# Keys with the four column positions innermost, ACT's norm in the second pair of a row, and a loop of two samples a turn (two turns) in place of one sample (five turns)

## What is computed

```
x = x + window_attention(group_norm(x))
x = x + lif(group_norm(x) @ W.T + b)          # over the 8 samples as time steps
# window_attention: windows of 8 x 8 positions, 16 heads of 16 channels
qkv  = part @ qkv_w.T + qkv_b ;  q = q * 16 ** -0.5
attn = softmax(q @ k.T + bias[rel_index] + mask)
out  = attn @ v
# group_norm: 32 groups of 8 channels, mean and variance over a sample's positions
# lif: v = v + (h - v) / 2 ; s = (v >= 1) ; v = v * (1 - s) ; output s
```

## Time and profile before

| | |
|---|---|
| median of 3 runs | 545.47 us (545.28 to 548.49) |
| the profiled execution | 546.64 us; its span 544.9 us |
| busy PE (matmul), PEld (weight load) | 434.2, 403.4 us |
| busy DVE, ACT, POOL | 398.2, 377.4, 280.3 us |
| queue of SP's DMAs | 154272 packets, 64.52 MB, 46.4% of 16 engines |
| packets under 512 bytes | 124978 of 155272 |
| granted TensorE clock | mean 0.962 of full speed |

### The profile page before, as it was taken

How to read it: one execution, slowest core, us unless ns; L and a number is a source line. 1 busy time by engine, 2 the same in 40 slices (tenths; PEclk the granted TensorE clock), 3 DMA queues, 4 the chain that set the end, 5 groups by cost and what they waited for, 6 DMA issues and landing times.

```text
span 544.9 us, 20474 instructions
## 1 busy us (share of the span) xinstructions
PE 434.2 (80%) x7912; PEld 403.4 (74%) x7912; DVE 398.2 (73%) x838; ACT 377.4 (69%) x863; POOL 280.3 (51%) x382
## 2 busy tenths in 40 slices
PE   0056658889878986988698879889988887889997
PEld 0056558878868886978698779778888776778886
DVE  5753757777776877677767767778877676588897
ACT  2353657878886887678778867788888786756551
POOL 6163456556654766475647654765685556640000
PEclk9996979999998999899989988999999998899999
DMA  7232534556554555455545654565555453023333
GB/s 204 67 81 65 140 75 107 142 142 155 138 139 109 141 138 137 109 128 142 138 114 133 139 131 112 129 140 134 123 118 119 111 125 80 2 78 136 135 137 135
DMA packets 155272, 65.78 MB, mean 121 GB/s; under 512 B 124978, under 2 KB 142644, under 8 KB 155188
## 3 DMA queue, kind: packets, MB, share of 16 engines
q1 hardware_dynamic: 154272, 64.52, 46.4%
q10 hardware_dynamic: 916, 0.01, 0.1%
HBM read 39.33 MB, written 25.17 MB: 118 GB/s over the span
## 4 chain that ended last, share of the span: by engine, by line
PE 38%; SPq 21%; ACT 11%; DMA 10%; issue 9%; DVE 8%; ACTq 1%; POOL 0%; DVEq 0%; POOLq 0%
SPq L317 12%; SPq L311 7%; DMA k_stack<-k_spill0lo 4%; PE pv_ps L1050 4%; PE proj_ps L939 3%; DMA k_stack<-k_spill1lo 3%; PE proj_ps L940 3%; PE proj_ps L941 3%; PE score_ps L1026 3%; PE score_ps L1016 3%; PE proj_ps L926 3%; PE pv_ps L926 3%; PE score_ps L926 3%; ACT xn L493 2%; ACT v_hi L529 2%
## 5 line engine op out<-in xcount | busy, mean ns | idle before, releaser
L454 POOL TENSOR_TENSOR p_lo<-probs,p_hi 128x512 f16<-128x512 f32 x128 | 146.4, 1165 | 147.3 <-ACT p_hi L608 122.9
L1016 PE MATMUL score_ps<-q_stack,k_stack 96*128 96x64 f16 x1024 | 88.1, 197 | 50.5 <-ACT max_rows L598 39.2
L1016 PEld LDWEIGHTS score_ps<-q_stack,k_stack 96*128 96x128 f16 x1024 | 74.2, 100 | 56.8 <-ACT max_rows L598 47.7
L785 DVE TENSOR_REDUCE neg_max<-max_ps 128x16 f16<-128x1024 f32 x64 | 78.4, 1225 | 42.9 <-PE max_ps L996 41.3
L607 ACT ACTIVATE probs<-score_ps 128x512 f32<-128x512 f32 x128 | 76.9, 601 | 38.4 <-PE score_ps L1026 37.6
L779 DVE TENSOR_TENSOR v_lo<-proj_ps,v_hi 64x256 f16<-64x256 f32 x128 | 54.2, 423 | 59.3 <-ACT v_hi L529 58.4
L939 PE MATMUL proj_ps<-xn_hi,w_hi 128*128 128x256 f32 x256 | 76.8, 300 | 10.7 <-DVE w_lo L738 7.2
L1012 PE MATMUL score_ps<-both_parts,bias_k 128*128 128x64 f16 x1024 | 80.8, 197 | 0.0
L608 ACT ACTIVATE p_hi<-score_ps 128x512 f16<-128x512 f32 x128 | 77.3, 604 | 0.0
L1012 PEld LDWEIGHTS score_ps<-both_parts,bias_k 128*128 128x128 f16 x1024 | 72.8, 100 | 2.8
L940 PE MATMUL proj_ps<-xn_lo,w_hi 128*128 128x256 f32 x256 | 73.8, 288 | 0.0
(11 more groups left out here) (131 smaller groups left out, 1211.4 us busy)
## 6 DMA issues: line engine op xcount, KB each, us to landing
xc<-in_x_dram SPq DMA_DIRECT2D x32, 256.0 KB, 3.1
out_dram<-xc SPq DMA_DIRECT2D x32, 256.0 KB, 2.2
q_stack<-q_spill0hi SPq DMA_DIRECT2D x32, 128.0 KB, 2.6
k_stack<-k_spill0hi SPq DMA_DIRECT2D x64, 64.0 KB, 3.5
q_stack<-q_spill1hi SPq DMA_DIRECT2D x32, 128.0 KB, 2.6
k_stack<-k_spill1hi SPq DMA_DIRECT2D x64, 64.0 KB, 3.4
q_spill0hi<-q_flat SPq DMA_DIRECT2D x16, 128.0 KB, 2.4
k_spill0hi<-k_flat SPq DMA_DIRECT2D x16, 128.0 KB, 1.9
```

The source lines that it names most:

```text
L454: pool.tensor_tensor(p_lo[p][:, quads, :, :].rearrange("p g w i -> p (g w i)"), probs[:, quads, :, :].rearrange("p g w i -> p (g w i)"), p ...
L785: dve.tensor_reduce(neg_max[:, :].rearrange("p (m n) -> p m n", m=2)[:, :, 0:8], max_ps[:, :, :].rearrange("p m (n j) -> p m n j", j=WS), ...
L1016: pe.matmul(dst, k_stack[slot][0:96, 2 * mid + q, at, :], q_stack[slot][0:96, 2 * mid + q, at, :], start=False, stop=False)
```

## The change

Three things are changed. `k_flat` and `k_stack` have the window column innermost: `k_stack` becomes [128, 4, 2, 128, 4], ACT (`k_high`) and DVE (`k_low`) write their outputs with a step of 4 elements (8 bytes), the pieces of the k DMAs become 64 keys x 4 windows, and PE reads k with that step. ACT's `normalise` goes from the end of the second pair to its start: one half before `q_high`, the other between `q_high` and `k_high`. `run` writes out samples 0, 5, 6 and 7 and loops over samples 1 to 4, two samples a turn.

```diff
-        k_stack = [sb(f"k_stack{i}", [128, QUADS, HALVES * WCOLS, 128], f16) for i in range(2)]
+        k_stack = [sb(f"k_stack{i}", [128, QUADS, HALVES, 128, WCOLS], f16) for i in range(2)]
...
-            with eng.Fori(1, SAMPLES - 2) as s:
-                for k in range(BODY):
-                    body(s * BODY + k, s * WROWS + k // 2, k, s)
-            for s in (SAMPLES - 2, SAMPLES - 1):
+            with eng.Fori(0, (SAMPLES - 3) // 2) as twice:
+                for s in (twice * 2 + 1, twice * 2 + 2):
+                    for k in range(BODY):
+                        body(s * BODY + k, s * WROWS + k // 2, k, s)
+            for s in range(SAMPLES - 3, SAMPLES):
...
+        def keys_of(buf, part):
+            if buf is k_flat:
+                return buf[:, part, :].rearrange("p (h j w) -> p h w j", h=HALVES, w=WCOLS)
+            return buf[:, part, :].rearrange("p (h w j) -> p h w j", h=HALVES, w=WCOLS)
...
-                    sp.dma_start(k_stack[slot][rows, quads, :, e * WS:(e + 1) * WS],
-                                 k_spill[slot][part][e * D:(e + 1) * D, quads, :].rearrange("d g (n j) -> d (g n) j", j=WS))\
+                    sp.dma_start(k_stack[slot][rows, quads, :, e * WS:(e + 1) * WS, :].rearrange("r g h j w -> r (g h) (j w)"),
+                                 k_spill[slot][part][e * D:(e + 1) * D, quads, :].rearrange("d g (h n) -> d (g h) n", h=HALVES))\
...
-            def normalise(row, sample, slot, norm, done):
-                wait(act, xn_lo_done, done - 1)
-                normed(xn[slot], row, sample, norm).then_inc(xn_done, 1)
+            def normalise(row, sample, slot, norm, done, halves=range(HALVES)):
+                if 0 in halves:
+                    wait(act, xn_lo_done, done - 1)
+                last = normed(xn[slot], row, sample, norm, halves)
+                if HALVES - 1 in halves:
+                    last.then_inc(xn_done, 1)
...
-                act.activation(k_flat[:, 0, :], proj_ps[:, 1, :], ACT.Copy).then_inc(k_hi_done, 1)
+                act.activation(keys_of(k_flat, 0), keys_of(proj_ps, 1), ACT.Copy).then_inc(k_hi_done, 1)
...
-                if p == 1 and not is_last_row(row, 2):
-                    q_high(row + 3)
-                    k_high(row + 3)
+                if p == 1:
+                    sample = s + (k // 2 + 3) // WROWS
+                    for h in range(HALVES):
+                        if not is_last_row(row, 3):
+                            normalise(row + 3, sample, nxt % 2, sample + 1, row + 3, (h,))
+                        if not is_last_row(row, 2):
+                            (q_high, k_high)[h](row + 3)
...
-                if p == 1 and not is_last_row(row, 3):
-                    sample = s + (k // 2 + 3) // WROWS
-                    normalise(row + 3, sample, nxt % 2, sample + 1, row + 3)
...
-                dve.tensor_tensor(k_flat[:, 1, :], proj_ps[:, 1, :], k_flat[:, 0, :], ALU.subtract).then_inc(k_lo_done, 1)
+                dve.tensor_tensor(keys_of(k_flat, 1), keys_of(proj_ps, 1), keys_of(k_flat, 0), ALU.subtract).then_inc(k_lo_done, 1)
...
                                 last = pe.matmul(max_ps[queries, mid, col:col + 128], q_stack[slot][rows, 2 * mid + q, at, :],
-                                                 k_stack[slot][rows, 2 * mid + q, at, :],
+                                                 k_stack[slot][rows, 2 * mid + q, h, :, 2 * (k % 2) + w],
...
-                                pe.matmul(dst, k_stack[slot][0:96, 2 * mid + q, at, :], q_stack[slot][0:96, 2 * mid + q, at, :],
+                                pe.matmul(dst, k_stack[slot][0:96, 2 * mid + q, h, :, 2 * p + w], q_stack[slot][0:96, 2 * mid + q, at, :],
```

More of the change, by code:

```diff
@@ L390, in clear_stack @@
             def clear_stack(slot):
-                return pool.memset(k_stack[slot][:, :, :, :].rearrange("p g n j -> p (g n j)").bitcast(f32), 0.0)
+                return pool.memset(k_stack[slot][:, :, :, :, :].rearrange("p g h c w -> p (g h c w)").bitcast(f32), 0.0)
             clear_stack(0).then_inc(const_step, 1)
@@ L486, in _, with normed @@
                                   allow_slow_non_contiguous=True).then_inc(b_loaded, 16)
-            def normed(dst, row, sample, norm):
+            def normed(dst, row, sample, norm, halves=range(HALVES)):
                 act.wait_ge(norm_ready, norm)
-                for h in range(HALVES):
+                for h in halves:
                     col = bass.ds(sample * HALVES + h, 1)
```

## The result

| | before | after |
|---|---|---|
| median of the runs, us (lowest to highest) | 546.98 (545.28 to 554.74), 4 runs | 576.65 (572.83 to 578.21), 4 runs |
| ratio of after to before, 95% interval | | 1.052 [1.044, 1.060] |
| the profiled execution, us (its span) | 546.64 (544.9) | 577.36 (575.6) |
| mean granted clock of TensorE | 0.962 | 0.935 |

The change costs 5.2%. 541.5 us was predicted, 524 to 566 the range: the result lies 35 us above the forecast and 11 us outside the range. Now and then an execution falls into a slower state (554.74 us is one); the ratios leave such runs out, the medians in us do not.

A forecast was written before the change was run, and what follows sets the result against it. A PE-ACT ring was taken to bound rows of 12.25 us, with SP's issues nearly as tight and turn ends third. Terms -31.3 + 32.1 + 17 - 9.9 - 11.8 = -3.9 us gave 541.5 us against the median, range 524 to 566.

The forecast's parts named there:

- The wait that moves with the norm: Pairs with k = 3, samples 0 to 6: ACT waits for POOL's shift, PE gets its copy later; +32.1 us.
- The clock after such a wait: PE at 1.2 GHz for 5.8 us behind each new wait, 2.4 us lost each time, seven times; +17 us.
- The loop: Turn ends: one of four is left, three at 3.3 us each are saved; -9.9 us.
- The norm leaves the first pair's stretch: First pair of a row: ACT's path to the copy of the maxima shortens by 1.16 us, 27 times; -31.3 us.
- SP's ring: SP's issues, called nearly as tight as the PE-ACT ring: eight k DMAs a row at 0.63 us, a q read 0.42.
- k's layout: SP's k DMAs: pieces grow from 128 to 512 bytes, an issue falls to 0.42 us, k waits go; -11.8 us.
- SP stays out of the way of rows of 11.1 us: With cheaper k issues, saving 1.6 us a row, SP was not to hold up the shortened rows.
- The step of 8 bytes: ACT's and DVE's k writes, PE's reads: taken as 0; upper bound for ACT 0.44 us a row, 13 us.
- Rival 2: ACT's strided k write dear before the copy of the maxima, 554.7 us, or PE's weight loads slower, 572 us; 17%.
- Rival 3: k DMAs get no cheaper, issues stay 0.63 us, rows stay 12.25 us; 585 us, 575 called fairer; 7%.

The follow-up runs named there:

- experiment 1: old_layout: the changed kernel with k's old layout and old write, norm placement and loop kept; 570.62 us, ratio 1.039 to the kernel before.
- experiment 4: Kernel before with the new loop and the norm at the second pair's start except at k = 3, old layout; 541.20 us, ratio 0.989.
- experiment 5: The changed kernel with the norm left at the second pair's end at k = 3, new layout and loop kept; 545.79 us, ratio 0.995.
- experiment 3: The kernel before with only the loop of two samples a turn; 544.59 us, ratio 0.994.
- experiment 9: experiment 6 with four k DMAs of 32 partitions instead of eight of 16, output not the reference's; 503.04 us, ratio 0.922.
- experiment 6: experiment 4 with 512-byte pieces in k's DMAs, ACT, DVE and PE contiguous, output not the reference's; 527.60 us, ratio 0.964.
- experiment 7: experiment 4 with only ACT's and DVE's writes of k in 8-byte steps, output not the reference's; 560.47 us, ratio 1.029.
- experiment 10: experiment 5 with ACT and DVE writing k contiguously and reading PSUM in steps of 256 bytes; 526.26 us, ratio 0.964.
- experiment 12: The ladder: experiment 4 with ACT, DVE and PE operations at several steps added behind its end; one run, only its rows count.
- experiment 8: experiment 4 with only PE's reads of k in 8-byte steps, output not the reference's; 540.87 us, ratio 0.990.

## Why the prediction was wrong

By its own steps:

- *The wait that moves with the norm*: right in place, number and size. 7 waits of ACT, PE's 3.21 and 4.83 to 5.00 us against 2.7 and 4.9, 32.9 us in all against 32.1.
- *The clock after such a wait*: the mechanism is shown, seven times, the size was too high. It is slow for 31 us in all and not for 7 x 5.8 = 41, so 31 x 0.42 = 13 us in place of 17; the rows behind the waits give 12. Wait and clock together were measured by experiments 1 and 4 and by the result and experiment 5: 29.4 and 30.9 us. For the same comparison the prediction's terms give 32.1 + 17 - 7 x 1.16 = 41. The clock's size explains 4 or 5 of the 10 to 12 us between them. Some of the rest is that SP catches up during the wait: the waits for k are 34.1 us in experiment 4 and 25.9 in old_layout, 14.3 in experiment 5 and 11.9 in the changed kernel.
- *The loop*: one turn end is left, as predicted, and 3.4 us [1.0 to 5.7] came of the 9.9. The waits for k that appeared in their place are in experiment 3.
- *The norm leaves the first pair's stretch*: the wait in the first pair went, the time did not. 23 us were due from the rows without the shift's wait, 3.4 came (experiment 4). The step that failed is not this one but the next, on which it rested: with SP's ring out of the way rows last 11.05 us (experiment 9).
- *k's layout*: wrong. "I take 0.42, as the pieces are what differs" failed: with pieces of 512 bytes an issue of k takes 0.60 us, and "SP stays out of the way of rows of 11.1 us", which hung on it, failed too. k's DMAs also have 16 partitions and q's 32, but with 32 partitions an issue of k still took 0.60 us; there were half as many, and the time fell by 24.6 us (experiment 9). What makes an issue of q, with pieces of 4 KB, cheaper (0.42 us) no run settled. The pieces brought 13.6 us by themselves (experiment 6), with the landing of a read down from 3.3 to 2.7 us, which no term counted; the waits for k, which the term of 11.8 us had gone, were still 23.6 us in that kernel. The 11.8 came out in size, 13.6, and not by its mechanism: that is luck. The norm's 23 and these 11.8 together promised 35 us and brought 17; with half the DMAs it was 42.
- *The step of 8 bytes*: wrong, and with the norm's 20 missing us the largest mis-sized term: 0 taken, 19.3 and 19.5 us measured (experiments 7 and 10; 22 and 17 by the ratios). "8 bytes are much nearer to contiguous than 128" treated the step as a distance, and the row that served as the upper bound was a read. A write of 16-bit values with this step costs 1.34 us in place of 0.60, 0.74 us more where the upper bound was 0.44, and in experiment 12 a write with a step of 4 elements takes 1322 ns, a read 660. Rival 2 had the mechanism and its place right, with a price too small (0.74 x 30 = 22 us, not 13); DVE's doubled `k_low`, which delays the spill and so SP's chain, it did not have. PE's side of it was there and cost no time: the matmuls of L1007 are longer, 291 ns against 216, the loads of L1027 114 ns against 100, half of what rival 2 supposed, and experiment 8 puts both at nothing, give or take 6 us, in a kernel where PE waits for k.
- *Rival 3*: its condition came true, an issue of k stayed at 0.60 us and the long issues stayed, and its 575 us is next to 576.65. That is luck: it had no price for the writes (about 19 us), took the gain of the pieces (13.6) as nothing, and had the wait for the shift and its clock 10 us too dear.

The statement in the Trainium skill (SBUF — State Buffer, the note on cachelines in Door 1: The DMA port swizzle) that 16-bit data can be strided by up to 8 elements for free was weighed in the prediction. The ladder agrees with it for reads by ACT and DVE up to 4 elements (660 and 692 ns against 629 and 692), and not at 8 (1112 and 1061). For writes it fails, on ACT from 2 elements on (746 against 597), on both engines clearly at 4 (1322 and 1316 against 597 and 691); and PE's moving columns take twice as long at 4 (3.71 against 1.82 us). The measurement decides: here the note holds for reads by ACT and DVE up to a step of 4.

What the change does, then, from medians, on about 548 us: three turn ends -3.4, the norm's move in the rows without a shift to wait for -3.4, the pieces -13.6, the writes with a step +19.3, PE's step nothing, and 1 us by which the three parts of the layout differ from their sum: 545.8 (experiment 5). The wait for the shift and its clock add 30.9: 576.7. The same terms in the forecast are -9.9, -23.2, -11.8, 0, 0 and +41, so it was too low by 6.5 for the loop, 19.8 for the norm and 19.3 for the writes, and too high by 10 for the wait. Each of these differences is known to some 4 to 8 us, since the ratios are known to 0.4 to 1%.

## What to carry to other kernels

Before moving an instruction up an in-order queue, look up which of its inputs is the latest in *any* turn of the loop: one row in four that waits 5 us for another engine outweighs 1.2 us in each of the others. When a transposed layout is wanted, put the step on the side that reads and write contiguously: here the order of iteration alone was worth 17 to 19 us, and the read side was the projection's f32 tile. And before a shorter stretch of one engine is counted as gained, add up the next ring (here SP: instructions times 0.6 us): its cost went with the number of DMAs, and pieces of 512 in place of 128 bytes hardly changed it (598 against 626 ns).

## What the runs showed of the hardware that was not expected

- Writes by ACT and DVE of 16-bit values pay for a step, on ACT from 2 elements on: 0.60, 0.75, 1.32, 2.48 us on ACT and 0.69, 0.73, 1.32, 2.47 on DVE for steps of 1, 2, 4 and 8 and 512 values in each of 128 partitions. A write of f32 with steps of 1, 2 and 4 took ACT 0.60, 0.63 and 1.08 us. Reads cost next to nothing up to a step of 4 (0.63, 0.63 and 0.66 us on ACT, 0.69 three times on DVE) and 1.11 and 1.06 us at 8.
- A read of the f32 projection tile by ACT or DVE in steps of 256 bytes is free: 597 and 691 ns, as contiguous.
- PE's moving columns with a step of 4 go at half the rate in the ladder, one matmul behind the other at a granted clock of 1.00: 541.59 to 543.43 against 543.43 to 547.14 for 32 matmuls, 1.84 against 3.71 us. In the kernel 1024 such matmuls, with 64 rows and 64 weights each, kept PE busy for 14 us more and the time did not change (experiment 8).
- An issue by SP of a read of k takes 0.63 us with pieces of 128 bytes and 0.60 with 512, and 0.60 whether it covers 16 or 32 partitions.
